# A 2-D FFT mixing kernel: the small blocks' own product as four 64x64 tiles, and small results laid out by pair

## What is computed

```python
xf = rfft2(x, axes=(1, 2), norm='ortho')          # (4, 128, 65, 768), 8 blocks of 96 channels
o1r = relu(xr @ w1[0] - xi @ w1[1] + b1[0]);  o1i = relu(xi @ w1[0] + xr @ w1[1] + b1[1])
o2r = o1r @ w2[0] - o1i @ w2[1] + b2[0];      o2i = o1i @ w2[0] + o1r @ w2[1] + b2[1]
out = irfft2(softshrink(o2r) + 1j * softshrink(o2i), s=(128, 128), norm='ortho') + x
```

## Time and profile before

| | |
|---|---|
| median of three runs | 5403.48 us |
| the profiled execution | 5402.93 us, span 5400.7 us |
| PE busy | 98% of the span, 44672 passes |
| DVE, ACT, POOL busy | 68%, 41%, 12% |
| mean granted TensorE clock | 0.999 of full speed |

### The profile page before, as it was taken

One profiled execution on the slowest core, in us unless ns is written; L12 is line 12 of the kernel. 1 busy time (PEld: TensorE's weight loads), 2 busy tenths in 40 slices (PEclk: granted clock), 3 DMA queues, 4 the chain that ended last, 5 costly groups with the idle time before them and its releaser, 6 DMA issues.

```text
span 5400.7 us, 113004 instructions
## 1 busy us (share of the span) xinstructions
PE 5305.9 (98%) x44672; PEld 4318.5 (80%) x44672; DVE 3683.3 (68%) x5859; ACT 2213.5 (41%) x3457; POOL 626.7 (12%) x420
## 2 busy tenths in 40 slices
PE   6999999999999999999999999999999999999999
PEld 5887878878788787888878888888878888787787
DVE  5676676676676766767667676676766766766765
ACT  3443434434344443444434443434434344343443
POOL 0110011110111101111011110011110111101111
PEclk9999999999999999999999999999999999999999
DMA  3331333312333123331133321333312333123311
GB/s 102 95 82 33 85 95 95 97 32 70 95 95 99 45 55 96 95 99 51 49 95 95 99 67 39 90 95 99 83 38 75 95 99 95 40 61 95 99 48 48
DMA packets 1065700, 421.23 MB, mean 78 GB/s; under 512 B 1062816, under 2 KB 1062944, under 8 KB 1065120
## 3 DMA queue, kind: packets, MB, share of 16 engines
q1 hardware_dynamic: 1060384, 411.62, 28.6%
q10 hardware_dynamic: 4736, 1.60, 0.1%
HBM read 210.26 MB, written 201.33 MB: 76 GB/s over the span
## 4 chain that ended last, share of the span: by engine, by line
issue 88%; POOL 11%; POOLq 0%; DVE 0%
POOL x L795 11%; POOLq L794 0%; POOLq L798 0%; DVE x L747 0%; POOLq L795 0%; POOLq L807 0%
## 5 line engine op out<-in xcount | busy, mean ns | idle before, releaser
L795 POOL TENSOR_TENSOR x<-shrink_or_v,x 128x480 f32<-128x480 f32 (+1 forms) x416 | 626.4, 1506 | 4766.3 <-DVE shrink_or_v L740 4726.2
L712 DVE TENSOR_TENSOR shrink_or_v<-ps,wts 128x768 f32<-128x768 f32 (+1 forms) x544 | 501.8, 922 | 950.1 <-PE ps L484 950.1
L484 PE MATMUL ps<-wts,hbig 128*128 128x192 f32 x4160 | 821.6, 340 | 0.0
L484 PEld LDWEIGHTS ps<-wts,hbig 128*128 128x128 f32 x4160 | 661.0, 189 | 122.2 <-issue 122.2
L591 ACT COPY zbig<-ps 128x512 f32<-128x512 f32 (+1 forms) x544 | 309.3, 569 | 966.5 <-PE ps L418 966.5
L402 PE MATMUL ps<-tab,ring_h 128*128 128x128 f32 x6144 | 694.6, 276 | 4.1
L402 PEld LDWEIGHTS ps<-tab,ring_h 128*128 128x128 f32 x6144 | 688.5, 192 | 10.2 <-DVE ring_h L766 10.2
L389 PE MATMUL ps<-tab,ring_a 128*64 128x128 f32 x6144 | 680.4, 273 | 3.2 <-ACT ring_a L555 3.2
L390 PE MATMUL ps<-tab,ring_a 128*63 128x128 f32 x6144 | 680.4, 273 | 0.0
L389 PEld LDWEIGHTS ps<-tab,ring_a 128*64 128x64 f32 x6144 | 671.9, 137 | 7.2 <-ACT ring_a L555 4.2
L390 PEld LDWEIGHTS ps<-tab,ring_a 128*63 128x63 f32 x6144 | 671.8, 136 | 0.0
(11 more groups left out here) (54 smaller groups left out, 6705.7 us busy)
## 6 DMA issues: line engine op xcount, KB each, us to landing
x<-in_x SPq DMA_DIRECT2D x128, 1536.0 KB, 12.3
out<-x SPq DMA_DIRECT2D x352, 480.0 KB, 4.7
out<-x SPq DMA_DIRECT2D x32, 432.0 KB, 4.1
wts<-in_mix SPq DMA_DIRECT2D x16, 513.0 KB, 3.6
out<-x SPq DMA_DIRECT2D x32, 240.0 KB, 4.3
out<-x SPq DMA_DIRECT2D x32, 192.0 KB, 4.4
ydg<-row ACTq DMA_DIRECT2D x32, 48.0 KB
yedge<-row ACTq DMA_DIRECT2D x32, 0.8 KB
```

Source lines behind the costliest of these rows:

```text
L484: mm = pe.matmul(o, hbig[u % 2][:, k * H:(k + 1) * H], mix_part("w2_big"), start=False, stop=True, skip_group_check=True)
L712: dve.tensor_tensor(parts(v), d, b2, ALU.add).then_inc(bias_done, 1)
L795: pool.tensor_tensor(xs[p][:, a:b, :], ucopy[g % 4][:, 0:b - a, :], mirror(xs[p], a, b), ALU.add).then_inc(plus_ready, 1)
```

## The change

The product small to small is taken out of `mix1_whole` and becomes `mix1_quarters`, after `mix1_columns`: four matmuls of 64x64 weights, one for each (i, k), 128 columns each. Their inputs lie on the partitions of i, their outputs on the partitions of k, so the four stand on the four quarters of the array. The small result is therefore laid out by pair: partitions by k, and i selects the bank (4 or 5). To match, `mix1_columns` becomes four matmuls of 128 columns, the small relu reads two banks, `mix2_rows` takes its rows by k, the second layer's result has banks by k (6 and 7), and `shrink` writes ydg in the order in which it lies. `merge` moves to bank 2 and waits for the last `hid_ready`. Cut to its core:

```diff
-        ZBIG_BANK, ZSMALL_BANK, BIG_BANK, SMALL_BANK, OUT_BANK, E_BANK = 0, 1, 2, 4, 5, 7
+        ZBIG_BANK, ZSMALL_BANK, BIG_BANK, SMALL_BANK, OUT_BANK = 0, 1, 2, 4, 6
+        E_BANK = BIG_BANK
...
-                    r = small_rows(u)
-                    pe.matmul(ps[0:r, SMALL_BANK, 0:n], mix_part("w1_small_small")[0:r, 0:r], zsmall[u % 2][0:r, 0:n],
-                              start=True, stop=False)
...
+                def small_out(i, k):
+                    return ps[k * SMALL:(k + 1) * SMALL, SMALL_BANK + i, 0:H]
...
-                    for i, a, b in halves:
-                        mm = pe.matmul(ps[i * SMALL:(i + 1) * SMALL, SMALL_BANK, 0:n],
-                                       mix_part("w1_big")[:, BIG:2 * CB], zbig[u % 2][:, a:b], start=False, stop=True)
+                    for i in range(kinds(u)):
+                        for k in range(len(GROUP_PAIRS[u])):
+                            pe.matmul(small_out(i, k), mix_part("w1_big")[:, BIG:2 * CB],
+                                      zbig[u % 2][:, i * n + k * H:i * n + (k + 1) * H], start=True, stop=False)
+
+                def mix1_quarters(q, u):
+                    for k in range(len(GROUP_PAIRS[u])):
+                        for i in range(kinds(u)):
+                            half = slice(i * SMALL, (i + 1) * SMALL)
+                            mm = pe.matmul(small_out(i, k), mix_part("w1_small_small")[half, half],
+                                           zsmall[u % 2][half, k * H:(k + 1) * H], start=False, stop=True)
                     mm.then_inc(small_mixed, 1)
...
+                    for i in range(kinds(u)):
+                        for k in range(len(GROUP_PAIRS[u])):
+                            half = slice(k * SMALL, (k + 1) * SMALL)
+                            pe.matmul(ps[:, out_bank(u, k), i * 2 * CB:(i + 1) * 2 * CB],
+                                      hsmall[u % 2][half, i * H:(i + 1) * H],
+                                      mix_part("w2_small")[half], start=i == 0, stop=False, skip_group_check=True)
...
                     pe.wait_ge(shrunk, NU * q + EDGES + 1)
+                    pe.wait_ge(hid_ready, NU * q + NU)
...
                                 mix1_columns(q, it - 1)
+                                mix1_quarters(q, it - 1)
                                 mix1_rows(q, it - 1)
...
+                    act.activation(hsmall[u % 2][0:r, 0:m * H].rearrange("p (i n) -> p i n", i=m),
+                                   ps[0:r, SMALL_BANK:SMALL_BANK + m, 0:H], ACT.Relu, bias=b1[0:r, 1:2])
...
+                    dst = ydg[:, lo:lo + 2 * m * (ne - first), :].rearrange("p k c -> p (k c)")
+                    dve.tensor_tensor(dst, v[:, n:], c[:, n:], ALU.subtract).then_inc(shrunk, 1)
```

More of the change, by code:

```diff
@@ L315, in small_rows, with kinds @@
         def small_rows(u):
-            return BIG if odds(u) else SMALL
+            return SMALL * len(GROUP_PAIRS[u])
+        def kinds(u):
+            return 2 if odds(u) else 1
         def odd_rows(g):
@@ L432, in fwd_small @@
                     mm.then_inc(zsmall_done, 1)
-                def halves_of(u):
-                    n = len(evens(u)) * H
-                    return n, [(0, 0, n)] + ([(1, n, 2 * n)] if odds(u) else [])
                 def mix1_whole(q, u):
@@ L442, in mix1_whole @@
                         pe.wait_ge(hid_ready, NU * q + u)
-                    n, halves = halves_of(u)
-                    for i, a, b in halves:
-                        pe.matmul(ps[:, BIG_BANK + i, 0:n], mix_part("w1_big")[:, 0:BIG], zbig[u % 2][:, a:b],
-                                  start=True, stop=False)
-                    r = small_rows(u)
-                    pe.matmul(ps[0:r, SMALL_BANK, 0:n], mix_part("w1_small_small")[0:r, 0:r], zsmall[u % 2][0:r, 0:n],
-                              start=True, stop=False)
@@ L451, in mix1_columns @@
-                def mix1_columns(q, u):
-                    n, halves = halves_of(u)
-                    for i, a, b in halves:
-                        mm = pe.matmul(ps[i * SMALL:(i + 1) * SMALL, SMALL_BANK, 0:n],
-                                       mix_part("w1_big")[:, BIG:2 * CB], zbig[u % 2][:, a:b], start=False, stop=True)
+                    n = len(evens(u)) * H
+                    for i in range(kinds(u)):
+                        pe.matmul(ps[:, BIG_BANK + i, 0:n], mix_part("w1_big")[:, 0:BIG],
+                                  zbig[u % 2][:, i * n:(i + 1) * n], start=True, stop=False)
@@ new lines, in small_out @@
+                def small_out(i, k):
+                    return ps[k * SMALL:(k + 1) * SMALL, SMALL_BANK + i, 0:H]
+                def mix1_columns(q, u):
+                    n = len(evens(u)) * H
+                    for i in range(kinds(u)):
+                        for k in range(len(GROUP_PAIRS[u])):
+                            pe.matmul(small_out(i, k), mix_part("w1_big")[:, BIG:2 * CB],
+                                      zbig[u % 2][:, i * n + k * H:i * n + (k + 1) * H], start=True, stop=False)
@@ L472, in mix2_rows @@
                         pe.wait_ge(bias_done, NU * q + min(u, NU - 2))
[L473 to L478, removed]
+                    for i in range(kinds(u)):
+                        for k in range(len(GROUP_PAIRS[u])):
[3 more added lines that the diff above has]
+                                      mix_part("w2_small")[half], start=i == 0, stop=False, skip_group_check=True)
                 def mix2_whole(q, u):
                     n = len(evens(u))
[L482 to L485, removed]
+                    for k in range(n):
+                        for i in range(kinds(u)):
+                            mm = pe.matmul(ps[:, out_bank(u, k), i * 2 * CB:(i + 1) * 2 * CB],
+                                           hbig[u % 2][:, (i * n + k) * H:(i * n + k + 1) * H], mix_part("w2_big"),
+                                           start=False, stop=True, skip_group_check=True)
                     mm.then_inc(mix2_done, 1)
@@ L538, in _ @@
                         mix1_columns(q, NU - 1)
+                        mix1_quarters(q, NU - 1)
                         mix1_rows(q, NU - 1)
@@ L595, in relu @@
                         act.wait_ge(mix2_done, NU * q + u - 1)
-                    n, r = len(evens(u)) * H, small_rows(u)
+                    n, r, m = len(evens(u)) * H, small_rows(u), kinds(u)
                     b1 = mix_part("b1")
                     act.wait_ge(small_mixed, NU * q + u + 1)
-                    act.activation(hsmall[u % 2][0:r, 0:n], ps[0:r, SMALL_BANK, 0:n], ACT.Relu, bias=b1[0:r, 1:2])
+                    act.activation(hsmall[u % 2][0:r, 0:m * H].rearrange("p (i n) -> p i n", i=m),
+                                   ps[0:r, SMALL_BANK:SMALL_BANK + m, 0:H], ACT.Relu, bias=b1[0:r, 1:2])
                     act.wait_ge(big_mixed, NU * q + u + 1)
@@ L692, in copy_small @@
                         dve.wait_ge(big_mixed, NU * q + u - 1)
-                    n, r = len(GROUP_PAIRS[u]) * H, small_rows(u)
+                    n, r = len(GROUP_PAIRS[u]) * H, SMALL * kinds(u)
                     dve.tensor_copy(zsmall[u % 2][0:r, 0:n], ps[0:r, ZSMALL_BANK, 0:n]).then_inc(zsmall_ready, 1)
                 def shrink(q, u):
-                    ne, no = len(evens(u)), len(odds(u))
-                    halves = 2 if no else 1
-                    n = halves * ne * 2 * CB
+                    ne, m = len(evens(u)), kinds(u)
+                    n = ne * m * 2 * CB
                     v, c = biased[u % 2][:, 0:n], clamped[u % 2][:, 0:n]
                     def parts(t):
-                        return t.rearrange("p (i k c) -> p i k c", i=halves, c=2 * CB)
-                    d = ps[:, out_banks(u), 0:ne * 2 * CB][:, 0:halves].rearrange("p i (k c) -> p i k c", c=2 * CB)
-                    b2 = mix_part("b2").rearrange("p (i k c) -> p i k c", i=1, k=1).broadcast_to([128, halves, ne, 2 * CB])
+                        return t.rearrange("p (k i c) -> p k i c", i=m, c=2 * CB)
+                    d = ps[:, out_banks(u), 0:m * 2 * CB][:, 0:ne].rearrange("p k (i c) -> p k i c", c=2 * CB)
+                    b2 = mix_part("b2").rearrange("p (k i c) -> p k i c", i=1, k=1).broadcast_to([128, ne, m, 2 * CB])
                     dve.wait_ge(mix2_done, NU * q + u + 1)
@@ L717, in shrink @@
                     if u == EDGES:
-                        dve.tensor_tensor(edge[:], parts(v)[:, :, 0, :], parts(c)[:, :, 0, :], ALU.subtract)
+                        dve.tensor_tensor(edge[:], parts(v)[:, 0], parts(c)[:, 0], ALU.subtract)
                         first = 1
[L720 to L723, removed]
+                    lo, n = 2 * evens(u)[first], first * m * 2 * CB
+                    dst = ydg[:, lo:lo + 2 * m * (ne - first), :].rearrange("p k c -> p (k c)")
+                    dve.tensor_tensor(dst, v[:, n:], c[:, n:], ALU.subtract).then_inc(shrunk, 1)
                 def add_halves(q, p, g):
```

## The result

The changed kernel takes **5378.75 us** (median of five runs, 5378.41 to 5379.68), the kernel before 5403.69 (five runs beside it): 24.9 us less, a ratio of 0.9954 with a 95% interval of 0.9941 to 0.9968. The forecast was 5379.

A forecast was written before the change was run, and what follows sets the result against it. PE's issue order in the mixing was taken as the bound: 0.38 + 0.004 - 0.432 = -0.048 us a unit, times 512 = -24.6 us, from 5402.93 to 5378.3, plus 0.55 for the runs' median: 5379 us, range 5368 to 5390.

The forecast's parts named there:

- The bound: In the mixing, PE's issue order is the time; a unit goes from 5.99 us to 5.94, nothing else becoming late.
- Removed, 0.432: In a mixing unit, the old small-to-small group's two passes of 256 columns go, 0.432 us; the shape change behind it stays.
- The gaps of the weight loader: The weight loader idles 0.33 us before L430's loads, where the array shape changes, and elsewhere runs ahead.
- The quarters, 0.38: The new four-tile phase of a unit costs 0.38 us; low end 0.36, high end 0.58.
- drain and first load: At each change of array shape: 0.09 us plus the first load, 0.05 for 64 columns.
- The columns, +0.004: In a unit, four matmuls of 128 columns replace two of 256: 4 rounds of 0.109 for 2 of 0.216, +0.004 us.
- ACT, shrink, merge, dispatch at nothing: Small relu on ACT (at most 0.1 us more), shrink on DVE, merge's wait and 28 matmuls for 23 add nothing.
- The sum: Over 512 mixing units: 0.38 + 0.004 - 0.432 = -0.048 us a unit, -24.6 us in all.
- Pairs only: Rival: the quarters run only two at a time, +0.152 us a unit, 5481 us; chance 0.08.
- loads one after another: Rival: the quarters' four first weight loads run in series, +0.08 us a unit, 5445 us; chance 0.05.
- In order: Rival: passes start strictly in program order, only neighbours overlap in the quarters, +0.26 us a unit, 5537 us; chance 0.02.
- each tile takes its matmuls as soon as it is free: On PE, tiles queue apart; a tile's first matmul is late only by dispatch, 0.02 us for three further tiles.

The follow-up runs named there:

- experiment 2: Each quarter's matmul issued twice, so the small product is added twice, against the changed kernel: 5497.58 us, 118.8 more.
- experiment 4: The quarters put ahead of the columns in the changed kernel, same matmuls with one change of shape more: 5455.96 us, 77.2 more.
- experiment 3: Only two of the four quarters issued, half of the small product left out, against the changed kernel: 5372.27 us, 6.5 less.
- experiment 6: The columns' four matmuls issued tile by tile (upper, upper, lower, lower) where the changed kernel alternates: 5404.79 us, 26.0 more.
- Experiment 5: shrink's last step walks ydg and its operands by i first again, as the kernel before does, in the changed kernel: 5378.80 us.
- experiments 6 to 8: Against the changed kernel: columns tile by tile, 5404.79 us; columns upper, lower, lower, upper, 5378.86 us; fwd_small's four matmuls tile by tile, 5381.79 us.
- experiment 10: Changed kernel with small-to-big product and second layer's rows as 64x64 tiles (all units but the last two for the latter), waits before the columns: 5274.31 us, 104.4 less.

## Why the prediction was right

- *The bound.* PE's issue order in the mixing, one unit 5.94 us: as forecast. Nothing else became late. Outside the mixing, the inverse lines keep PE busy for 21.70 us of a q in both kernels.
- *Removed, 0.432.* L447 to L436 fell from 1.39 to 0.96.
- *The gaps of the weight loader.* The prediction has it idle ahead of L430 and running ahead elsewhere. It idles at the other changes of shape too (0.39 and 0.22, above). That speaks for the price that was worked out, not against it.
- *The quarters, 0.38.* 0.37 to 0.38 in the timeline, and 196.6 / 512 = 0.384 by leaving them out, 0.378 without the last unit's 3 us. Its terms, each by itself: two rounds 0.218 (experiment 2), drain and first load 0.151 (experiment 4, forecast 0.146), and 0.0127 for the third and fourth tile, so 0.019 for three further ones at the same rate (experiment 3, forecast 0.02). The Trainium skill (TensorE: Matmul & The Clock Gate, Part 3, the span model) gives about 4 ns for a tile where this kernel shows 6; an estimate by that figure puts the forecast some 4 us lower, and so 4 us too low.
- *The columns, +0.004.* 0.54 against 0.53. Right in size, but for a reason that I had not seen: they are free in the order in which they stand, alternating. Tile by tile they cost 0.05 more a unit (experiment 6), which is the whole gain.
- *ACT, shrink, merge, dispatch at nothing.* Experiment 5 for shrink, the rows on DVE and ACT above for the cover. The merge and the banks had no experiment of their own; the sum leaves nothing for them.
- *The sum.* 0.38 + 0.01 - 0.43 by the timelines, to 0.01 each, and 0.01 is 5 us over 512 units. The terms were right, but that the forecast of 5379 met 5378.75 to 0.3 us is closer than they carry, and partly luck.
- *The rivals.* Pairs only falls with experiments 2 and 3, loads one after another with the quarters' first passes above, which wait together. In order: the Trainium skill (the same page, What overlaps and what doesn't) has matmuls start strictly in program order. The trace after shows the contrary again, where `fwd_small` of the last unit has work for one half only (timeline of PE, kernel after):

```profile
987.99 0.32 PE L436 MATMUL ps<-tab,ydg 128*64 128x128 f32 x1
988.00 0.32 PE L457 MATMUL ps<-zbig,wts 128*64 128x128 f32 x1
988.15 0.27 PE L436 MATMUL ps<-tab,ydg 128*64 128x128 f32 x1
```

A pass of L457 starts ahead of the second pass of L436, which stands before it in the program. L436 has the upper half in use until that second pass has run, so the pass of L457 can only be for the lower half, and its matmul stands behind one of L457 for the upper half: by this reading a whole matmul is overtaken, too. But the sentence of the prediction that "each tile takes its matmuls as soon as it is free" went too far. Experiment 6 refutes it, and the slot theory (handed out in program order, one ahead for a tile) agrees with experiments 6 to 8.

## What to carry to other kernels

Where TensorE issues small fp32 matmuls without waits, count the changes of array shape in its loop before counting the work: here each cost 0.09 us (0.11 behind four tiles) and an unhidden first load (0.05 for 64 columns, 0.10 for 128), so that the change kept 0.05 us of the 0.21 that its arithmetic saved (0.43 to 0.22). Recutting other small products to the shape that is already set (experiment 10) gave four times what the four tiles themselves gave. And when tiles run side by side, deal the matmuls out in turn: two in a row for one tile ahead of the other tile's first, right behind a busy group, cost 26 us here.

## What the runs showed of the hardware that I had not expected

- The order of matmuls among tiles matters although tiles run apart: upper, upper, lower, lower costs 26 us over upper, lower, upper, lower, with one pass a unit at 323 ns in place of 272; upper, lower, lower, upper costs nothing.
- Recutting a group to the shape of the one before gains only if a change of shape goes. With the rows as 64x64 tiles a plain unit kept its 1.66 us, since the change and its first load of 128 columns came back one group later. The first unit of a q, where no 64x128 group follows, went from 1.01 to 0.81.
- Four tiles with 256 and 192 columns run at full pace as well: 16 passes of 192 columns take 0.76 with the drain behind them (0.75 for the 8 passes on two tiles before, drain included).
